# Loading x and adj transposed by DMA, one float per element, in a two-layer graph kernel

## What is computed

```python
hi = x @ W1[:H];  hj = x @ W1[H:]
h = relu(hi[:, None, :] + hj[None, :, :] + b1)        # every pair i, j
y = layernorm(h @ W2 + b2) * gamma + beta             # every pair i, j
x1 = _layernorm(x + einsum('ij,ijh->ih', adj, y))

Wh = x1 @ W_w.T + W_b
s = (Wh @ a_w[:C])[:, None] + (Wh @ a_w[C:])[None, :] + a_b
e = exp(s) * adj
out = _layernorm(x1 + (e / e.sum(1)) @ x1)
```

## Time and profile before

| | us |
|---|---|
| median of 3 runs | 2457.67 |
| lowest and highest | 2455.99, 2457.86 |
| profiled execution | 2456.72 |
| its span, first to last instruction | 2454.9 |
| PE busy | 2390.1 (97%) |
| ACT busy | 2231.9 (91%) |
| DVE busy | 2117.0 (86%) |
| POOL busy | 2022.4 (82%) |
| mean granted clock of PE | 0.994 |

### The profile page before, as it was taken

One profiled execution on the slowest core, in us unless ns is written; L12 is line 12 of the kernel. 1 busy time (PEld: TensorE's weight loads), 2 busy tenths in 40 slices (PEclk: granted clock), 3 DMA queues, 4 the chain that ended last, 5 costly groups with the idle time before them and its releaser, 6 DMA issues.

```text
span 2454.9 us, 181527 instructions
## 1 busy us (share of the span) xinstructions
PE 2390.1 (97%) x73792; PEld 2063.3 (84%) x73792; DVE 2117.0 (86%) x17817; ACT 2231.9 (91%) x3841; POOL 2022.4 (82%) x1227
## 2 busy tenths in 40 slices
PE   8999999999999999999999999999999999999997
PEld 7888888878888888888888878888888888888885
DVE  7888888888888888888888888888888888888887
ACT  7999999989999899998999989999899998999996
POOL 7888888878888788888888878888788887888884
PEclk9999999999999999999999999999999999999999
DMA  0000000000000000000000000000000000000000
GB/s 20 11 13 15 11 15 16 10 17 12 14 16 10 17 16 10 16 13 14 15 10 15 15 12 15 10 15 16 11 16 11 14 15 11 15 16 10 15 11 8
DMA packets 48687, 33.45 MB, mean 14 GB/s; under 512 B 6208, under 2 KB 47808, under 8 KB 47808
## 3 DMA queue, kind: packets, MB, share of 16 engines
q1 hardware_dynamic: 46512, 21.12, 3.1%
q10 hardware_dynamic: 1296, 0.20, 0.0%
HBM read 17.11 MB, written 4.19 MB: 9 GB/s over the span
## 4 chain that ended last, share of the span: by engine, by line
PE 83%; ACT 9%; issue 4%; DVE 3%; POOL 0%; ACTq 0%; DMA 0%; DVEq 0%
PE y_ps L529 61%; PE agg_ps L574 18%; ACT h L288 5%; ACT y L270 3%; PE prep_ps L529 2%; DVE squares L515 2%; PE tail_ps L529 1%; ACT beta_part L328 1%; ACT ln_v L317 1%; PE att_ps L529 1%; DVE q L515 0%; POOL h L259 0%; ACT rstd L322 0%; DMA beta_rows<-in_L_gnn_beta_dram 0%; ACTq L367 0%
## 5 line engine op out<-in xcount | busy, mean ns | idle before, releaser
L259 POOL TENSOR_TENSOR h<-bT,aT 128x1024 f32<-128x1024 f32 x1024 | 1950.2, 1916 | 376.0 <-PE y_ps L529 354.8
L529 PEld LDWEIGHTS y_ps<-w_pair,h 128*32 128x32 f32 x65536 | 1837.8, 110 | 289.8 <-issue 208.2
L515 DVE CUSTOM_DVE_ANT_0 squares<-y_ps,y 128x128 bf16<-128x128 f32 x8192 | 1849.1, 286 | 265.9 <-ACT y L270 257.6
L529 PE MATMUL y_ps<-w_pair,h 128*32 128x128 f32 x65536 | 1973.3, 274 | 42.8 <-issue 25.3
L270 ACT ACTIVATE y<-y_ps 128x508 f32<-128x508 f32 x2048 | 1163.5, 596 | 164.7 <-PE y_ps L529 159.5
L288 ACT ACTIVATE h<-h 128x1024 f32<-128x1024 f32 x1024 | 1084.8, 1059 | 26.6 <-issue 14.9
L515 DVE DVE_READ_ACCUMULATOR2_ANT q<- 128x1 f32 x8192 | 679.6, 83 | 0.0
L574 PE MATMUL agg_ps<-y,wz 128*32 128x512 f32 x4096 | 548.7, 594 | 0.0
L574 PEld LDWEIGHTS agg_ps<-y,wz 128*32 128x32 f32 x4096 | 137.3, 110 | 3.8 <-issue 3.8
L451 DVE SCALAR_TENSOR_TENSOR o_sb<-agg_ps,part,o_sb 128x128 f32<-128x128 f32 x192 | 66.5, 346 | 0.2
L233 POOL TENSOR_TENSOR wz<-adjT,rstd 128x128 f32<-128x128 f32 x64 | 33.5, 523 | 34.2 <-ACT rstd L322 34.2
(11 more groups left out here) (90 smaller groups left out, 725.2 us busy)
## 6 DMA issues: line engine op xcount, KB each, us to landing
x_in<-in_x_dram SPq DMA_DIRECT2D x64, 64.0 KB, 2.3
adj_in<-in_adj_dram SPq DMA_DIRECT2D x64, 64.0 KB, 2.5
x_res<-in_x_dram SPq DMA_DIRECT2D x64, 64.0 KB, 2.0
adj_res<-in_adj_dram SPq DMA_DIRECT2D x64, 64.0 KB, 2.4
out_dram<-x_out SPq DMA_DIRECT2D x64, 64.0 KB, 1.6
w<-in_L_gnn_W_dram ACTq DMA_DIRECT2D x1, 64.0 KB, 2.3
w1a<-in_L_gnn_W_dram SPq DMA_DIRECT2D x1, 64.0 KB, 2.2
w1b<-in_L_gnn_W_dram SPq DMA_DIRECT2D x1, 64.0 KB, 2.2
```

The source lines that it names most:

```text
L259: nc.gpsimd.tensor_tensor(h[:, u % HRING].rearrange("k (r g) s -> k r g s", g=GROUPS), bT[:, p, :].unsqueeze(1).unsqueeze(1).broadcast_to( ...
L515: last = nc.vector.tensor_tensor_reduce(out=squares[:, k % YRING, n, :], in0=y_ps[k % YRING][:, n, :], in1=y[:, p, i, :], scale=1.0, scala ...
L529: last = nc.tensor.matmul(dst[cols], lhsT[:, cols], rhs, start=True, stop=True, tile_position=(0, g * GROUP))
```

## The change

`x` and `adj` are no longer loaded as they lie. SP's DMAs read them with the two dimensions swapped, straight into `xT` and `adjT`, and each float is an element of its own. `x_in`, `adj_in`, PE's `prep_transposes` and ACT's `prep_copies` with their three semaphores go. `xT` gets a second buffer. `adjT` of graph t+1 is loaded in slot t when POOL has read the buffer (`w_ready`, `adjS_ready`), and ahead of `x_res` and `adj_res`. At the start w1a, w1b and b1c stand ahead of the first adj.

```diff
-        xT = sb("xT", [H, S])
+        xT = sb("xT", [H, 2, S])
...
-                sp.dma_start(x_in[:, b, :], x[b]).then_inc(x_loaded[b], 16)
-                sp.dma_start(adj_in[:, b, :], adj[b]).then_inc(adj_loaded[b], 16)
+                sp.dma_start(xT[:, b, :], x[b].rearrange("s h -> h s"), allow_slow_non_contiguous=True).then_inc(x_loaded[b], 16)
                 if b == 0:
...
+                sp.dma_start(adjT[:, b, :], adj[b].rearrange("i j -> j i"), allow_slow_non_contiguous=True).then_inc(adj_loaded[b], 16)
...
-                    sp.wait_ge(xT_ps_s, t + 1)
-                    sp.dma_start(x_in[:, p, :], x[bass.ds(t + 2, 1)].rearrange("o s h -> (o s) h")).then_inc(x_loaded[p], 16)
-                    sp.wait_ge(adjT_ps_s, t + 1)
-                    sp.dma_start(adj_in[:, p, :], adj[bass.ds(t + 2, 1)].rearrange("o s h -> (o s) h")).then_inc(adj_loaded[p], 16)
+                    sp.wait_ge(ab_ps_s, t + 1)
+                    sp.dma_start(xT[:, p, :], x[bass.ds(t + 2, 1)].rearrange("o s h -> h (o s)"), allow_slow_non_contiguous=True).then_inc(x_loaded[p], 16)
+                if gather and not (isinstance(t, int) and t + 1 >= B):
+
+                    sp.wait_ge(w_ready, t)
+                    sp.wait_ge(adjS_ready, t)
+                    sp.dma_start(adjT[:, 1 - p, :], adj[bass.ds(t + 1, 1)].rearrange("o i j -> j (o i)"), allow_slow_non_contiguous=True).then_inc(adj_loaded[1 - p], 16)
...
-                pool.wait_ge(adjT_sb_s, t)
+                pool.wait_ge(adj_loaded[1 - p], nth16(half, p, -1))
...
-                    if prep and u == 7:
-                        prep_copies(t + 1, early + 1)
-                        copy(adjT[:, 1 - p, :], prep_ps[:, 1, :]).then_inc(adjT_sb_s, 1)
...
-            def prep_transposes(b, p, loads, later):
+            def prep_products(b, p, loads, later):
+
                 pe.wait_ge(x_loaded[p], loads)
                 if later:
 
                     pe.wait_ge(ab_sb_s, b)
-                mm(prep_ps[:, 0, :], x_in[:, p, :], ident[:]).then_inc(xT_ps_s, 1)
-                pe.wait_ge(adj_loaded[p], loads)
-                mm(prep_ps[:, 1, :], adj_in[:, p, :], ident[:]).then_inc(adjT_ps_s, 1)
-
-            def prep_products(b):
-
-                pe.wait_ge(adjT_sb_s, b + 1)
-                mm(prep_ps[:, 2, :], w1a[:], xT[:])
-                mm(prep_ps[:, 3, :], w1b[:], xT[:]).then_inc(ab_ps_s, 1)
+                mm(prep_ps[:, 2, :], w1a[:], xT[:, p, :])
+                mm(prep_ps[:, 3, :], w1b[:], xT[:, p, :]).then_inc(ab_ps_s, 1)
```

More of the change, by code:

```diff
@@ L91, in gnn_pair_kernel @@
         epsc = sb("epsc", [S, 1])
-        x_in, adj_in = sb("x_in", [S, 2, H]), sb("adj_in", [S, 2, S])
         x_res, adj_res = sb("x_res", [S, 2, H]), sb("adj_res", [S, 2, S])
@@ L135, in gnn_pair_kernel @@
             [sem(f"{n}_{p}") for p in range(2)] for n in ("x_loaded", "adj_loaded", "xres_loaded", "out_stored"))
-        xT_ps_s, adjT_ps_s, adjT_sb_s = sem("xT_in_psum"), sem("adjT_in_psum"), sem("adjT_in_sbuf")
         ab_ps_s, ab_sb_s = sem("ab_in_psum"), sem("ab_in_sbuf")
@@ L215, in _, with pair_weights @@
             nc.gpsimd.memset(epsc[:], EPS).then_inc(s_const, 1)
-            def pair_weights(t, p, early):
+            def pair_weights(t, half, p, early):
                 pool.wait_ge(rstd_ready, t)
-                pool.wait_ge(adjT_sb_s, t)
+                pool.wait_ge(adj_loaded[1 - p], nth16(half, p, -1))
                 if early >= 2:
@@ L239, in slot @@
                     if gather and u == POOL_WEIGHTS_UNIT:
-                        pair_weights(t, p, early)
+                        pair_weights(t, half, p, early)
                     if tail and u == POOL_RESIDUAL_UNIT:
@@ L270, in copy @@
                 return nc.scalar.activation(dst, src, ACT.Copy)
[L272 to L283, removed]
             def relu(t, u):
@@ L300, in _ @@
             nc.scalar.preload_act_table_set("natural_log_exp_and_others")
-            prep_copies(0, 0)
-            copy(adjT[:, 0, :], prep_ps[:, 1, :]).then_inc(adjT_sb_s, 1)
             for u in range(2):
@@ L536, in prep_transposes @@
                     pe.wait_ge(ab_sb_s, b)
-                mm(prep_ps[:, 0, :], x_in[:, p, :], ident[:]).then_inc(xT_ps_s, 1)
-                pe.wait_ge(adj_loaded[p], loads)
-                mm(prep_ps[:, 1, :], adj_in[:, p, :], ident[:]).then_inc(adjT_ps_s, 1)
-            def prep_products(b):
-                pe.wait_ge(adjT_sb_s, b + 1)
-                mm(prep_ps[:, 2, :], w1a[:], xT[:])
-                mm(prep_ps[:, 3, :], w1b[:], xT[:]).then_inc(ab_ps_s, 1)
+                mm(prep_ps[:, 2, :], w1a[:], xT[:, p, :])
+                mm(prep_ps[:, 3, :], w1b[:], xT[:, p, :]).then_inc(ab_ps_s, 1)
             pe.wait_ge(s_const, 6)
-            prep_transposes(0, 0, 16, False)
             pe.wait_ge(s_w, 16 * 9)
@@ L558, in _ @@
             pe.wait_ge(s_w1, 16 * 3)
-            prep_products(0)
+            prep_products(0, 0, 16, False)
             pe.wait_ge(s_setup_dve, 14)
@@ L588, in slot @@
                         mm(tail_ps[:, 1, :], oT_sb[:], w_back[:]).then_inc(f_ps_s, 1)
-                    if prep and u == 5:
-                        prep_transposes(t + 1, 1 - p, nth16(half, p, 1), True)
                     if prep and u == 9:
-                        prep_products(t + 1)
+                        prep_products(t + 1, 1 - p, nth16(half, p, 1), True)
                     if tail and u == 10:
```

## The result

| | us | ratio to before (95% interval) |
|---|---|---|
| before, median | 2456.83 | |
| after, median of 4 runs (2825.86 to 2832.97) | 2832.09 | 1.1522 (1.1504 to 1.154) |
| after, profiled execution; its span | 2825.86; 2824.0 | |

What follows compares the result with a forecast made beforehand. It took TensorE (PE), busy 97%, as the bound. Start 2.2 us, 128 transposed loads x 25.6 us, row tiles 41.4 us and end 57.1 us gave 3,377.5 us of span, 3,380 us in all (128 L + 103); range 2,425 to 5,550.

Steps and rivals of the forecast that it cites:

- PE's work, 27.7 us: Two transposes of the next graph leave PE, 0.44 us in 63 slots: at most 27.7 us; ACT's copies add nothing.
- One packet per float, 2.1 million: On queue q1 each transposed load becomes 16,384 packets of 4 bytes, near 2.1 million in all.
- Rival C: The load pattern is merged on the way, so not one packet per float; A's time, 2,431 us; chance 0.03.
- L: Time of one transposed load of 16,384 floats on the DMA engines: 9.0 to 42.2 us, taken as 25.6 us.
- The lower bound: DMA engines run small packets back to back, 1,024 of 8.8 ns on each: 9.0 us for one transposed load.
- The stall at adj_sum: DVE waits some 14 us per slot for adj_res behind adjT; DMA work sets a 51.9 us slot.
- The account of the queue's order: On SP's queue x_res and adj_res stand behind adjT, so DVE waits and the queue never runs dry.
- Rival A: DMA loads are hidden, 9.0 us each; PE's 27.7 us are gained: 2,431 us, -1.1%; chance 0.27.
- Rival B: Making descriptors on SP's queue sets the pace, 42.2 us per load: 5,505 us; chance 0.20, with anything over 35 us.
- Terms left at nothing: PE's saved 27.7 us, off the path, and instruction fetches lengthening loads by 42 to 668 us; both only widened the range.
- The clock: PE's clock may fall after idle gaps; cost nothing while the loss stays under some 14 us idle per slot.
- The sign: The whole kernel gets slower, by 37%; chances slower 0.73, faster 0.23, same 0.04.

Runs made afterwards that it cites:

- experiment 1: The changed kernel with x and adj loaded untransposed in runs of 512 bytes (row loads), waits and queue order kept: 2428.13 us, ratio 0.9881.
- experiment 2: The kernel before, its transposes kept, with both transposed loads added into buffers that nobody reads: 2816.14 us, ratio 1.146.
- six cuts: The changed kernel with each transposed load split by partitions into two or three parts, to use fewer DMA engines: 2551.06 to 2840.84 us.

## Why the prediction was right or wrong

- **PE's work, 27.7 us**: right in size, 28.7 us with ACT's copies and the waits (experiment 1). That the copies add nothing was not tested apart.
- **One packet per float, 2.1 million**: right, 2,127,280. Rival C is out.
- **L, the time of a load**: wrong, and the step on which the sum stood. I took 25.6 us, the middle; it is 10.8 us, and 9.4 at the best rate seen. The lower bound, 1,024 x 8.8 ns = 9.0 us from the packet's own duration, came near, in part by luck: in the long load the packets follow each other at 9.2 ns on an engine, but each one's record lasts 16.1 ns and they overlap. The rate of 61 and 67 packets in 0.1 us was that of short bursts, which the text called the weak point. The measured rate is up to 173.6 in 0.1 us, against 64. The estimate of 24.9 us from the Trainium skill, in the section cited there, misses in the same way: the measurement decides, and I let the two agree too easily. That section gives the 1,309 ns for bf16 and the factor of 19 for a large innermost stride at the destination; here the data are 4 bytes wide and lie side by side at the destination, so neither condition holds.
- **The stall at adj_sum, 52 us slots, chain on DMA**: did not happen, since L is under the break-even of 18.4 us. The account of the queue's order was right (x_res lands after 12.0 us, held behind adjT) but costs nothing: neither adj_sum nor x_beta waits for its load anywhere in the changed kernel.
- **Rival A** had an L near the measured one, 9.0 us, and the loads hidden, and its time, 2,431 us, is that of the row loads (2428.13). It misses the 404 us that a hidden load takes from PE.
- **Rival B**: out. SP issues 16,384 floats in 0.38 us, as fast as a row tile, and they move at up to 1,736 per us, where B had 128 in 0.33 us, or 388 per us.
- **Terms left at nothing**: here the real error of mechanism lies. The prediction took PE's own pace beside the loads as unchanged. Instruction fetches were named, 1.7% of 16 engines, only as something that could lengthen the loads. The effect runs the other way: the loads, 54% of the engines by their packets' time, hold up the fetches by some 2 us each, and PE's waits on issue grow from 32.7 us to 319.2. The clock was a cost of nothing because PE was to idle anyway; here PE sets the end, and the low clock is part of the 113 us by which its work grew.
- **The sign**: right by luck, for a wrong reason. By the forecast's own condition a load of 10.8 us is hidden and the change gains, as in rival A. 2832 us lies in the range, but by the sum's formula it would need L = (2832 - 103) / 128 = 21.3 us.

What stays open: the records show that a block's packet starts late and that PE goes on after it, but not the request itself, so where the fetch waits is inferred from the experiments. Which engines carry the fetches, why 11 engines are worse than 12, and what lengthens PE's work besides the clock, is not settled.

## What to carry to other kernels

An almost idle DMA system isn't free room for a kernel that TensorE bounds with many small matmuls: its code is moved by DMA too, here one 16 KB packet every 4 us with 0.5 us to spare. Before filling the DMA engines for several us at a time, look at q8's packets against PE's pace, and count PE's instructions between two waits on issue: multiples of 256 point at the fetches. If you must load so, leave some engines idle or cut and spread the loads. Fewer and wider matmuls took the waits away here but cost more than they gave, 2,641 us against 2,457. Measure the change's loads alone beside the old kernel (experiment 2): that shows a cost which no wait in the profile names.

## What the runs showed of the hardware

- 4-byte packets follow each other at 9.2 ns on a DMA engine at best; 16,384 floats from DRAM into 128 partitions take 10.8 us on 16 engines, two loads back to back.
- From DRAM to DRAM the same floats take about 200 us, nearly 20 times as long, and PE stands still for up to 104.7 us at a time meanwhile.
- PE's code arrives in packets of 16 KB, one per 256 records of PE. Where no floats are moved the next packet starts 0.8 us after PE begins a block, in the middle of a load 2.8 us after, and PE goes on 1.8 us after it has landed.
- A load on all 16 engines costs this PE about 3 us (404 / 128 = 3.2), and a flood of rows of 512 bytes 2.5 us (307 us for 124).
- The number of engines of a load follows the divisors of its partitions in all six cuts, and 12 in place of 16 took 233 of the 404 us away.
- PE's granted clock can fall to the lower level for a few us after a single gap, such as one of 3.68 us; all 47 falls in the changed kernel came after a gap of 2 us or more.
